# Layer-0 attention in a four-layer network: its first block merged and reordered, its end split between attention and expert mixture

## The reference, cut to what matters

```python
x = x + layernorm(attention0(layernorm(x)))    # 16 heads of 64, causal, 4 batches of 1024 tokens, width 128
x = x + layernorm(mixture0(layernorm(x)))      # 8 routed experts (top 2) + 2 shared, hidden 256
x = x + layernorm(attention1(layernorm(x)))
x = x + layernorm(soft_mixture1(layernorm(x)))

# attention0
q, k, v = (x @ w_q), (x @ w_k), (x @ w_v)      # 128 -> 1024 each, 16 heads
att = softmax(where(causal, q @ k.T / 8**2, -inf))
out = concat_heads(att @ v) @ w_u + b_u
# mixture0, for each expert e
y_e = (silu(x @ w1_e + b1_e) * (x @ w2_e + b2_e)) @ w3_e + b3_e
```

## Time and profile before

| | |
|---|---|
| median of 3 runs | 2395.15 us (2388.61 to 2400.78) |
| the profiled execution: its own time | 2398.1 us |
| its span, first to last instruction | 2396.4 us |
| PE, PE weight loads, DVE, ACT, POOL busy | 91%, 59%, 60%, 50%, 44% |
| mean granted TensorE clock | 0.963 |

### The profile page before, as it was taken

The page is one execution under the profiler, slowest core; times in us unless marked ns, Lnnn a source line. Parts: engine busy times, 40 slices in busy tenths (PEclk is TensorE's granted clock), DMA queues, the critical chain, the costliest instruction groups (busy, mean ns, idle before and its releaser), DMA issues. The chain is left out here.

```text
span 2396.4 us, 41419 instructions
## 1 busy us (share of the span) xinstructions
PE 2172.3 (91%) x15940; PEld 1419.7 (59%) x15940; DVE 1444.0 (60%) x3312; ACT 1206.1 (50%) x1788; POOL 1042.6 (44%) x980
## 2 busy tenths in 40 slices
PE   4999999999999999976999999689999998897787
PEld 3555565556555565535888888543444455565667
DVE  4687757776687757753666556546545555556533
ACT  2555535554465535531333323278777866664543
POOL 0777747777677757771323223423323321100001
PEclk8999999999999999997999999789999999899999
DMA  2000000000000000003000000000000000002001
GB/s 76 1 1 1 1 1 1 1 1 1 1 1 1 1 1 1 1 1 74 1 1 1 1 1 1 0 1 1 1 1 1 1 1 1 2 8 71 1 1 36
DMA packets 36328, 18.26 MB, mean 8 GB/s; under 512 B 16667, under 2 KB 33957, under 8 KB 36133
## 3 DMA queue, kind: packets, MB, share of 16 engines
q1 hardware_dynamic: 36132, 15.61, 2.6%
HBM read 13.50 MB, written 2.10 MB: 7 GB/s over the span
## 5 line engine op out<-in xcount | busy, mean ns | idle before, releaser
L343 POOL TENSOR_TENSOR a_first<-a_first,a_ring 128x512 f32<-128x512 f32 (+3 forms) x352 | 556.6, 1581 | 244.0 <-PE a_o_ps L521 206.6
L1843 ACT ACTIVATE g_probsT<-g_s_ps 128x1024 f32<-128x1024 f32 (+2 forms) x448 | 368.9, 869 | 144.1 <-PE g_s_ps L1712 89.6
L625 ACT ACTIVATE a_ring<-a_st 128x768 f32<-128x768 f32 (+1 forms) x256 | 228.6, 918 | 85.7 <-PE a_st L506 83.3
L698 DVE TENSOR_REDUCE a_part_max<-a_mx 128x2 f32<-128x1024 f32 x128 | 156.4, 1222 | 139.7 <-PE a_mx L472 138.2
L721 DVE RECIPROCAL a_row_inv<-a_row_inv 128x256 f32<-128x256 f32 x128 | 218.5, 1731 | 22.0 <-ACT a_row_inv L613 22.0
L521 PE MATMUL a_o_ps<-a_ring,a_v 128*64 128x512 f32 (+3 forms) x1280 | 226.6, 474 | 3.4 <-POOL a_ring L325 3.3
L1113 ACT ACTIVATE m_silu<-m_up,m_b 128x512 f32<-128x512 f32 x160 | 109.6, 688 | 223.8 <-PE m_up L1045 221.0
L1743 PE MATMUL g_o_ps<-g_probsT,g_values 128*32 128x512 f32 (+5 forms) x2688 | 213.6, 430 | 5.2 <-POOL g_probsT L1588 5.1
L1712 PE MATMUL g_s_ps<-g_qT,g_kT 64*128 64x512 f32 (+3 forms) x896 | 173.6, 435 | 27.7 <-ACT g_probsT L1843 22.0
L1588 POOL TENSOR_SCALAR_AFFINE_SELECT g_probsT<-g_probsT 128x512 f32<-128x512 f32 x128 | 88.0, 691 | 252.5 <-ACT g_probsT L1843 252.3
L472 PE MATMUL a_mx<-a_k_hi,a_q_hi 64*128 64x512 f32 (+3 forms) x768 | 146.8, 404 | 24.7 <-DVE a_largest L705 17.5
(11 more groups left out here) (318 smaller groups left out, 4363.6 us busy)
## 6 DMA issues: line engine op xcount, KB each, us to landing
m_w<-in_L_ffn_rw SPq DMA_DIRECT2D x2, 1024.0 KB, 8.5
s_w<-in_L_ffn_w SPq DMA_DIRECT2D x1, 2048.0 KB, 9.8
s_w<-in_L_ffn_w SPq DMA_DIRECT2D x4, 512.0 KB, 10.5
out_x<-x SPq DMA_DIRECT2D x8, 256.0 KB, 2.3
m_w<-in_L_ffn_rw SPq DMA_DIRECT2D x2, 512.0 KB, 5.5
x<-in_L_attn_x SPq DMA_DIRECT2D x1, 512.0 KB, 4.1
a_outT<-in_L_attn_w_q SPq DMA_DIRECT2D x1, 512.0 KB, 4.9
a_outT<-in_L_attn_w_k SPq DMA_DIRECT2D x1, 512.0 KB, 5.8
```

Source lines behind the costliest of these rows:

```text
L343: pool.tensor_tensor(total[:, h, q:q + w], total[:, h, q:q + w], probs_of(n, u)[:, h, off:off + w], ALU.add).then_inc(added, 1)
L625: act.activation(probs_of(n, u)[:, :, 0:w], st_ps[u % 2][:, :, 0:w], ACT.Exp).then_inc(exp_done, 1)
L698: last = dve.tensor_reduce(part_max[:, i, :], mx_ps[:], AX.X, ALU.max)
L1843: act.activation(out, src.rearrange("p k (j n) -> p k j n", j=at_once), ACT.Exp, scale=float(HD) ** -0.5).then_inc(exp_done, 1)
```

## The change

The constants' block and the prologue's block go; everything up to the end of the attention is one block. The mask `mask_kq`, which nothing read, goes with its DMA.

- SP loads x of batch 0 in two halves with a semaphore each, then the identity, w_k, w_q, w_v (a semaphore each), the masks, the rest. After the last projection SP loads the mixture's gate, up weights and biases (`MixtureStart.load`), into the place where the attention's split weights were.
- DVE's layer norm starts on the first half (`first_norm`), and takes the low parts of w_k and w_q between its steps; the low part of w_v is made by POOL.
- The two halves of the input are turned into separate banks (`st1`), the first projections alternate between `p_ps` and `o_ps`, each half of the input is waited for alone, and the order of the work before pair 0 is written out; units 0 and 1 of pair 0 stand in it.
- In the last batch the normalising and turning slots are used for the mixture's input of batch 0 (`inputs_of_phase`, `normalized`), so that the mixture's block starts without them.
- The last output product is `output_part`: 64 matmuls of 128 columns, in four places of the banks `st0` and `st1`, pairs 0 to 3 of the batch ahead of the last two `weigh`s, pair 4 ahead of the last row sums, pairs 5 to 7 after them.
- The last layer norm and residual of the attention go into window 0 of the mixture (`residual_parts`), and the first expert's weights are split in the attention's block.

```diff
--- before.py
+++ after.py
...
-    return [(n // PAIRS + 1, n % PAIRS - 4)] if (n % PAIRS, t) in ((4, 2), (5, 0)) and n // PAIRS + 1 < BATCH else []
+    return [(n // PAIRS + 1, n % PAIRS - 4)] if (n % PAIRS, t) in ((4, 2), (5, 0)) else []
...
-                        pe.wait_ge(norm.chain, NORM_STEPS)
+                        pe.wait_ge(ident_loaded, 16)
+                        pe.wait_ge(norm.chain, NORM_STEPS - 4 * (1 - c))
...
+                x_in = g.inputs["L0_attn_x"].rearrange("b (t p) n -> p (b t) n", p=P)
+                for half in range(2):
+                    blks = slice(half * NB // 2, (half + 1) * NB // 2)
+                    sp.dma_start(g.x[:, blks, :], x_in[:, blks, :]).then_inc(first_x_loaded[half], 16)
+                sp.dma_start(g.ident[:], g.inputs["c_ident"]).then_inc(ident_loaded, 16)
+                for n, name in ((1, "w_k"), (0, "w_q"), (2, "w_v")):
+                    sp.dma_start(raw[:, n, :], g.inputs["L0_attn_" + name]).then_inc(w_loaded[n], 16)
+                sp.dma_start(g.mask_wide[:, HALF - P:HALF], g.inputs["c_mask_qk"]).then_inc(mask_loaded, 16)
+                sp.dma_start(window[:], g.inputs["c_mask_window"]).then_inc(window_loaded, 16)
+                sp.dma_start(g.x[:, NB:NBLK, :], x_in[:, NB:NBLK, :]).then_inc(x_loaded, 16)
                 sp.dma_start(w_u[:], g.inputs["L0_attn_w_u"].rearrange("(t p) n -> p t n", p=P)).then_inc(x_loaded, 16)
                 sp.dma_start(b_u[:], g.inputs["L0_attn_b_u"].partition_broadcast(P)).then_inc(x_loaded, 16)
...
+                sp.wait_ge(qk_done, 4 * ALL_PAIRS)
+                sp.wait_ge(v_done, NB * HALVES)
+                g.mixture.load(nc, sp, g)
...
+                inverse_root(pool, norm, g.minus_half[:, 0:NB], 0)
+                pool.wait_ge(split_hi, 3)
+                pool.tensor_tensor(w_hl[:, 5, :], raw[:, 2, :], w_hl[:, 4, :].bitcast(F32), ALU.subtract).then_inc(split_v, 1)
...
-                    take_shared(qk_lo_done, 4 * m + k + 1)
+                    out = p_ps
+                    if m == 0:
+                        out = (p_ps, o_ps)[k % 2]
+                        if k >= 2:
+                            pe.wait_ge(qk_lo_done, k - 1)
+                        else:
+                            pe.wait_ge(split_lo, k + 1)
+                        shared[0] = (qk_lo_done, 3)
+                    else:
+                        take_shared(qk_lo_done, 4 * m + k + 1)
                     if m % PAIRS == 0:
-                        pe.wait_ge(xT_lo_done, 2 * b + 2)
+                        pe.wait_ge(xT_lo_done, 2 * b + half + 1)
...
+                        if blk == 0:
+                            pe.wait_ge(split_v, 1)
...
+                def output_part(t, p):
+                    b = BATCH - 1
+                    if p == 0:
+                        pe.wait_ge(exp_done, ALL_PAIRS * UNITS_A_PAIR - 1 + t // 2)
+                    pe.wait_ge(out_kept, 2 * (b * PAIRS + p) + t // 2 + 1)
+                    for i in range(2):
+                        blk = 2 * t + i
+                        last = pe.matmul(st_ps[t // 2][:, t % 2, i * P:(i + 1) * P],
+                                         outT[:, (b * PAIRS + p) % OUT_SLOTS, blk * P:(blk + 1) * P], w_u[:, p, :],
+                                         start=p == 0 and i == 0, stop=p == PAIRS - 1, skip_group_check=True)
+                    if p == PAIRS - 1:
+                        last.then_inc(y_done, 1)
+
+                def output_parts(pairs):
+                    for t in range(4):
+                        for p in pairs:
+                            output_part(t, p)
 
...
                 project(0, 0)
-                for n in range(-1, ALL_PAIRS + 1):
+                project(0, 1)
+                project_values(0, 0)
+                maxima(0, 0)
+                project_values(0, 1)
+                maxima(0, 1)
+                project(0, 2)
+                project_values(0, 2)
+                project_values(0, 3)
+                maxima(0, 2)
+                project(0, 3)
+                project_values(0, 4)
+                project_values(0, 5)
+                turn_maxima(0, 0)
+                maxima(0, 3)
+                project_values(0, 6)
+                maxima(0, 4)
+                project_values(0, 7)
+                score(0, 0)
+                maxima(0, 5)
+                score(0, 1)
+                maxima(0, 6)
+                project(1, 0)
+                maxima(0, 7)
...
+                for n in range(ALL_PAIRS):
                     running, m = 0 <= n < ALL_PAIRS, n + 1
                     for t in range(PHASES):
...
+                output_parts(range(4))
+                add_up_and_weigh(ALL_PAIRS, 0)
+                output_parts([4])
+                add_rows(ALL_PAIRS - 1, 1)
+                output_parts(range(5, PAIRS))
...
+                for n in (1, 0, 2):
+                    act.wait_ge(w_loaded[n], 16)
+                    act.activation(w_hl[:, 2 * n, :], raw[:, n, :], ACT.Copy).then_inc(split_hi, 1)
...
+                g.mixture.split_high(act, E_ROUTED)
...
+                def first_norm():
+                    parts = layernorm_parts(dve, chain, lambda blk: g.x[:, blk, :], lambda blk: x_norm[:, blk, :], norm, 0)
+                    dve.wait_ge(first_x_loaded[0], 16)
+                    parts[0]()
+                    parts[1]()
+                    dve.wait_ge(first_x_loaded[1], 16)
+                    for part in parts[2:5]:
+                        part()
+                    split_weights(1, 1)
+                    for part in parts[5:7]:
+                        part()
+                    split_weights(0, 2)
 
...
-                finished_last(BATCH - 1, 2 * BATCH - 1)
+                g.mixture.split_low(dve, E_ROUTED)
+                for part in range(4):
+                    add_bias(BATCH - 1, part)
...
+    def load(self, nc, sp, g):
+        for letter, e0, n, w_sem in (("s", E_ROUTED, E_SHARED, self.sw_loaded), ("r", 0, E_ROUTED, self.rw_loaded)):
+            for j in range(2):
+                sp.dma_start(self.w12[:, e0:e0 + n, j, :], g.inputs[f"L0_ffn_{letter}w{j + 1}"]
+                             .rearrange("e p n -> p e n")).then_inc(w_sem, 16)
+        sp.dma_start(self.gate_w[:], g.inputs["L0_ffn_gate_w"]).then_inc(self.small_loaded, 16)
+        sp.dma_start(self.gate_b[:], g.inputs["L0_ffn_gate_b"].partition_broadcast(P)).then_inc(self.small_loaded, 16)
+        sp.dma_start(self.iota[:], g.inputs["c_iota"].partition_broadcast(P)).then_inc(self.small_loaded, 16)
+        with nc.allow_non_contiguous_dma(reason="biases, one value per partition"):
+            for letter, e0, n, b_sem in (("s", E_ROUTED, E_SHARED, self.sb_loaded), ("r", 0, E_ROUTED, self.rb_loaded)):
+                for j in range(2):
+                    src = g.inputs[f"L0_ffn_{letter}b{j + 1}"].rearrange("e (h p) -> p (e h)", p=P)
+                    sp.dma_start(self.b12[:, j, e0:e0 + n, :].rearrange("p e h -> p (e h)"), src).then_inc(b_sem, 16)
+
...
-                        pe.wait_ge(xT_lo_done, b * 2 + half_of_unit(u) + 1)
-                    if b == 0 and half_of_unit(u) == 0 and h == 0:
-                        pe.wait_ge(w_split, place_of_unit(u) + 1)
-                    cols = cols_of(b, half_of_unit(u))
+                    if b and place_of_unit(u) == 0 and h == 0:
+                        pe.wait_ge(xT_lo_done, b * 2 + half_of_unit(u) - 1)
+                    if b == 0 and place_of_unit(u) and half_of_unit(u) == 0 and h == 0:
...
-                turn_input(0, 0)
                 for u in range(M_UNITS):
...
-                    if u == 0:
-                        turn_input(0, 1)
...
-                        ends = residual(b - 1) if b else []
+                        ends = residual(b - 1) if b else residual_parts(BATCH - 1, g.normed[:])
```

334 lines of the change are left out of this document (167 added, 167 removed).

## The result

| | before | changed |
|---|---|---|
| median of the first set of runs | 2393.89 us (4 runs, 2388.61 to 2400.78) | 2335.61 us (4 runs, 2332.60 to 2337.44) |
| ratio, 95% interval | | 0.9754, 0.9724 to 0.9784 |
| the profiled execution: span, mean clock | 2396.4 us, 0.963 | 2334.0 us, 0.976 |
| PE, DVE, ACT, POOL busy | 91%, 60%, 50%, 44% | 92%, 62%, 52%, 45% |

The kernel is 58.3 us faster by these runs, where 47.6 was forecast; the time of 2335.61 lies in the range, near its lower end. The gain lies above the 41 to 55 that the forecast gave its main case A. In a second set of runs the same kernel took 2337.92 against 2386.12, 48.2 less. Over all runs of both kernels (30 and 9) the medians are 2390.7 and 2337.4, 53.3 apart.

The account below looks back on a forecast made before the run. PE, busy 91% of the span, was taken as the bound, with gains where it stands still, chiefly start and seam. 9.8 + 2.9 - 3.5 + 38.4 = 47.6 off 2398.1, less 2.95 for the median: 2347.5 us, range 2334 to 2362.

Parts of the forecast that it names:

- main case A: Whole kernel: the summed forecast holds with each term within its near bounds, gain 41 to 55, 2340 to 2354; chance 0.66.
- First projection: Kernel start: first projection at 14.9 instead of 24.69, gain 9.8, with DVE held by POOL's subtraction; 12.7 if unheld.
- x in halves: Kernel start: only the last four statistics, half of 1.65 us, remain once all of x lands, ending at 5.8.
- To the second turning: First projection to second turning of the maxima: gain 2.9, from a separate bank and one value product fewer ahead.
- The wait of 1.6: Second projection, in its own bank, no longer waits for ACT's and DVE's copies of the first; 1.6 us gained.
- Input slots: Last batch of the attention: preparing the mixture's input in pairs 27 to 29 loses 3.5 us, bounds 2 and 5.
- The end: Attention's end to the mixture: first up-projection at 1084.4 instead of 1119.37, 35.0 us gained.
- The mixture's start: Mixture's unit 0 and window 0: 1.1 us from the second half's turning gone, 2.3 from less half clock.
- Rival D: Both broken stretches at clock 1.00, DVE not held by POOL: gain 55 to 62, about 2338; chance 0.12.
- C: Mixture's window 0: DVE becomes the bound with the moved layer norm, POOL stretching it; 6.5 back, 2354; chance 0.05.
- E: Slower than before: window 0 is entered after a short idle and stays at half clock; chance 0.02.
- F: Little change: x in halves lands no earlier, output matmuls delay the row sums; 36 remain, 2359; chance 0.02.

Follow-up runs that it names:

- wv_on_dve: Changed kernel with the subtraction for w_v's low part moved from POOL to DVE, behind the two low parts of the input; 2342.05 us in one run.
- the repeat: The changed kernel once more, nothing edited, 2337.92 us, ratio 0.9786; the kernel before was also repeated unedited, 2397.93 us in one run.
- no_input_slots: Changed kernel without normalising and turning the mixture's first input in the last batch, so window 0 works on stale input; 2342.08 us in one run.
- residual_at_end: Changed kernel with the attention's last layer norm and residual back behind its last bias instead of in window 0; median 2349.68 us, ratio 0.9832.

## Why the prediction came out as it did

**First projection (14.9 forecast, 15.17 measured).** Right in size and in its step: DVE stood for POOL's instruction, for 2.0 us, and `wv_on_dve` shows it. The load estimates were 0.4 us early (w_k's high part began at 6.90, not 6.5). What the forecast said of x in halves was wrong in weight: the statistics are not in the chain, w_k is.

**To the second turning, 2.9.** This is the term that was mis-sized. The forecast expected the second turning 31 us behind the first projection; it came 26.25 behind (25.73 in the repeat), against 33.84 and 35.19 in the two profiles of before, with the same matmuls between. That is 7.6 less (9.5 between the repeats) instead of 2.9, where the forecast's bound was 8. From there to the first exponential of pair 1 the changed kernel is 2.1 slower (28.09 against 26.04), which leaves 5.5 between the first two profiles and 7.9 between the repeats (61.22 and 53.28 us). The wait of 1.6 is right: the second projection begins 1.42 behind the first instead of 3.03. But the bank is worth 2.0 to 2.6 up to the turning, and most of the rest is the clock, which the forecast had left as it was.

It had read too little half clock there. The clock of 0.80 in the earlier trace rows counts the time up to 32.6 us as full, because the trace has no clock record before that; the matmuls say otherwise. Four of the first projections' lines in the kernel before:

```profile
28.31 0.63 PE L410 MATMUL a_p_ps<-a_xT_lo,a_w_hl 128*128 128x512 f32 x1
28.74 0.63 PE L410 MATMUL a_p_ps<-a_xT_hi,a_w_hl 128*128 128x512 f32 x1
...
34.66 0.39 PE L410 MATMUL a_p_ps<-a_xT_lo,a_w_hl 128*128 128x512 f32 x1
34.89 0.39 PE L410 MATMUL a_p_ps<-a_xT_hi,a_w_hl 128*128 128x512 f32 x1
```

They follow each other 0.43 us apart ahead of 32.6 and 0.23 behind it. Counted from the first projection to the second turning, with that beginning, the half-clock time is 21.6 us in the kernel before and 9.2 in the changed one (first profiles). Where PE sets the pace half of the difference is gained, so by estimate up to 6.2. The half-clock stretch of 10.2 us at 37.2 in the changed kernel lies across the turning, the one of before ahead of it, which fits the 2.1 given back. No run holds the clock fixed, so this share is argued and not shown.

**Input slots, 3.5.** Right: 3.52, and by `no_input_slots` 3.4 to 3.5.

**The end, 35.0 to the first up-projection.** Right, 35.2. From unit 7's end to the last bias 19.8 was forecast and 20.04 measured, and the single steps agree: 7.41 for the 32, 1.08 for the row sums at full clock, 2.05 for the last 8.

**The mixture's start, 3.4.** 2.3 in the first profile, 3.8 between the repeats: the clock, 0.87 against 0.64, with a stretch in one and none in the other. It was an estimate of half of 4.7, and the truth lies on both sides. The moved layer norm costs nothing (`residual_at_end`).

**What the sum lacked** is the clock further on. It took unedited code as unchanged. In the first pair of profiles that code was 13.5 us shorter: 4.4 in windows 2 and 3, in both pairs of profiles, and 9.1 behind the mixture, of which the repeat kept 3 to 5. The forecast of 47.6 is what the edited stretches gave (48.8), and what the second set of runs measured (48.2). That the first has 58.3 lies with the kernel before as much: its 30 runs go from 2378.38 to 2401.15, at mean clocks of 0.971 to 0.962 where these are listed, by and large the shorter the higher, while the 9 of the changed kernel stay in 2332.60 to 2338.58 at 0.975 to 0.978. Rival D, full clock in both broken stretches and no hold by POOL, gave the right total of the first set (2338) by luck: DVE was held, the front has its 10.2 us at half clock in every profile of the changed kernel, and 13.5 us of the difference between the first two profiles came from code that D says nothing of. C and E did not happen: PE stays at 20.00 of 20 in window 0 at clock 1.00. F's halves of x are indeed worth nothing, but w_k's earlier load carried the term.

Left open: the parts of the start's 9.5 us that no run undoes one by one (the order of the loads, the block in front, the weights' parts between the steps of the layer norm), and what brings the half-clock stretches behind the mixture, whose length sets the time there.

## What to carry to other kernels

A serial seam between two stages is paid in full and can be counted from the rows; here two of them, the start and the end, came out within half a us of the count. To do so, count the matmuls that can go under each wait, put ahead of a chain only what the chain needs, and let the rest fill the wait (pair 4's place cost 1.7 us). Look at what the neighbour engine gets to do beside the engine in the chain: POOL's subtraction, put there to relieve DVE, held DVE for its whole length. When most of a gain is made, compare several profiles of the same kernel before reading a few us in code that nobody edited.

## What the hardware showed that was not expected

- One DVE instruction with a single SBUF tensor input, 339 ns alone, took 2364 ns beside a POOL subtraction of 128x1024 that took 2.35 us and ended 0.08 us behind it. DVE instructions that had begun before POOL's were not lengthened (the one at 10.67, ahead of POOL's 10.86, took 338 ns). The hold was forecast from the earlier trace rows; that it takes one instruction in every profile was not.
- After 24 matmuls of 8 columns the granted clock fell to 1.2 GHz for one or two stretches in some executions and not in others, at the same code; 1.5 us each. Which of the two it is goes with where they begin among the steps in which the clock changes, without an exception in 56 places. The loss of one such stretch shifts the next place where it can happen, so an edit that saves 3.5 us (`no_input_slots`) can come out slower in a single run.
- The granted clock has no record for the first 16 to 33 us of these traces and is shown there as 1.00, while matmuls of 512 columns follow each other 0.43 us apart instead of 0.23.
- In window 0 of the changed kernel the steady units take 2.81 us instead of 2.75 in windows 1 to 3 and in the kernel before: the matmuls that read the turned input or the weights in their new places follow each other 0.234 us apart instead of 0.229. That is about 1 us in window 0. `residual_at_end` has the same 2.81, so the moved layer norm isn't the cause; the place of the operands was not tried.
